# A fused retention and mixture-of-experts layer: two experts' first weights loaded apart, and another order of step 0

## The reference

```python
x = x + attn(_layernorm(x), Wq, Wk, Wv, Wo)    # 8 heads of 16, chunks of 64, decaying state
x = x + ffn(_layernorm(x), Wg, W1, W2)         # 8 experts, hidden 256, the best 2 of each token

# attention, per chunk of 64 tokens and per head
attn = einsum('bhid,bhjd->bhij', qc, kc) * D
o = einsum('bhij,bhje->bhie', attn, vc) + einsum('bhid,bhde->bhie', qc * decay_q, S)
S = decay_s * S + einsum('bhjd,bhje->bhde', kc * decay_k, vc)

# experts, all computed densely, weighted by combine (zero but for two of eight)
h = square(relu(einsum('td,edh->teh', xt, W1)))
y = einsum('teh,ehd->ted', h, W2)
out = einsum('te,ted->td', combine, y)
```

## Time and profile before

| what | us |
|---|---|
| median of three runs | 295.58 |
| lowest and highest | 295.46, 301.28 |
| the profiled execution | 295.8 |
| its span, first to last instruction | 292.9 |
| TensorE busy in the span | 277.2 |
| mean granted clock of TensorE, of full speed | 0.987 |

### The profile page before, as it was taken

The page is one execution under the profiler, slowest core; times in us unless marked ns, Lnnn a source line. Parts: engine busy times, 40 slices in busy tenths (PEclk is TensorE's granted clock), DMA queues, the critical chain, the costliest instruction groups (busy, mean ns, idle before and its releaser), DMA issues.

```text
span 292.9 us, 8869 instructions
## 1 busy us (share of the span) xinstructions
PE 277.2 (95%) x3650; PEld 216.9 (74%) x3650; DVE 219.7 (75%) x569; ACT 176.4 (60%) x253; POOL 190.9 (65%) x152
## 2 busy tenths in 40 slices
PE   7977886999999999999999999999999998999995
PEld 5665465778787778877787777877787787888883
DVE  3746967796569967697569966699569858898883
ACT  2622629646675559746585549756585466686961
POOL 1113595977487786787487785787587874465752
PEclk9997799999999999999999999999999999999999
DMA  7119273004240240604241040304230051305301
GB/s 228 44 24 332 81 248 117 3 0 147 76 135 11 67 157 2 181 0 147 75 121 61 8 186 31 110 2 143 79 102 9 6 165 54 110 8 210 107 0 72
DMA packets 13704, 26.79 MB, mean 91 GB/s; under 512 B 1120, under 2 KB 6752, under 8 KB 13664
## 3 DMA queue, kind: packets, MB, share of 16 engines
q1 hardware_dynamic: 13664, 26.23, 28.0%
HBM read 24.00 MB, written 2.23 MB: 90 GB/s over the span
## 4 chain that ended last, share of the span: by engine, by line
POOL 36%; PE 28%; issue 24%; ACT 5%; DVE 3%; DMA 2%; POOLq 1%; DVEq 0%; ACTq 0%
POOL act_lo L1113 34%; PE h_ps L371 3%; POOL rstd L1085 2%; PE h_ps L373 2%; PE h_ps L372 2%; PE y_ps L398 2%; PE y_ps L392 2%; DMA scale<-w 2%; PE y_ps L393 2%; PE bank L511 1%; PE bank L522 1%; PE bank L432 1%; ACT act_sf L1008 1%; PE h_ps L415 1%; PE y_ps L347 1%
## 5 line engine op out<-in xcount | busy, mean ns | idle before, releaser
L1113 POOL TENSOR_TENSOR act_lo<-act_sf,act_hi 128x512 fp32r<-128x512 f32 x112 | 150.6, 1366 | 54.9 <-ACT act_sf L1008 54.6
L815 DVE SCALAR_TENSOR_TENSOR act_sf<-h_ps,scale 128x1024 f32<-128x1024 f32 x64 | 77.9, 1219 | 47.4 <-PE h_ps L373 21.1
L1001 ACT ACTIVATE act_hi<-act_sf 128x1024 fp32r<-128x1024 f32 x64 | 68.1, 1064 | 56.4 <-DVE act_sf L815 56.3
L1008 ACT ACTIVATE act_sf<-act_sf 128x1024 f32<-128x1024 f32 x64 | 67.3, 1052 | 0.0
L371 PE MATMUL h_ps<-x_hi,w_lo 128*128 128x512 f32 x128 | 54.9, 429 | 0.9 <-ACT act_sf L969 0.9
L373 PE MATMUL h_ps<-x_hi,w_hi 128*128 128x512 f32 x128 | 50.5, 394 | 0.0
L372 PE MATMUL h_ps<-x_lo,w_hi 128*128 128x512 f32 x128 | 50.4, 394 | 0.0
L392 PE MATMUL y_ps<-act_hi,w_lo 128*128 128x512 f32 x112 | 47.0, 420 | 0.0
L393 PE MATMUL y_ps<-act_hi,w_hi 128*128 128x512 f32 x112 | 44.0, 392 | 0.0
L398 PE MATMUL y_ps<-act_lo,w_hi 128*128 128x512 f32 x112 | 35.2, 396 | 0.1
L1085 POOL TENSOR_TENSOR rstd<-variance,minus_half 128x4 f32<-128x4 f32 x16 | 16.1, 1008 | 23.9 <-DVE variance L660 23.8
(11 more groups left out here) (143 smaller groups left out, 424.7 us busy)
## 6 DMA issues: line engine op xcount, KB each, us to landing
scale<-scratch SPq DMA_DIRECT2D x32, 512.0 KB, 4.1
x_t_in<-x_tr SPq DMA_DIRECT2D x8, 256.0 KB, 5.0
x_all<-x SPq DMA_DIRECT2D x8, 256.0 KB, 5.1
out<-out_sb SPq DMA_DIRECT2D x8, 256.0 KB, 4.3
scale<-w SPq DMA_DIRECT2D x1, 1024.0 KB, 5.4
cst<-constants SPq DMA_DIRECT2D x1, 288.0 KB, 4.7
cst<-constants SPq DMA_DIRECT2D x1, 256.0 KB, 2.7
cst<-constants SPq DMA_DIRECT2D x1, 232.0 KB, 5.0
```

Source lines behind the costliest of these rows:

```text
L815: nc.vector.scalar_tensor_tensor(out=act_s[:, u % 2], in0=h_ps[:, u % 2], scalar=0.0, in1=scale[:, f % 2, e].unsqueeze(1).to_broadcast([P, ...
L1001: nc.scalar.activation(act_hi[:, u % 4], act_s[:, u % 2], ACT.Square).then_inc(act_hi_ready, 1)
L1008: nc.scalar.activation(act_f[:, u % 2], act_s[:, u % 2], ACT.Square).then_inc(act_f_ready, 1)
L1113: nc.gpsimd.tensor_tensor(act_lo[:, u % 4, n], act_f[:, u % 2, n], act_hi[:, u % 4, n].bitcast(F32), ALU.subtract).then_inc(pool_low_ready, 1)
```

## The change

The load of `w1` is cut in two: experts 0 and 1 (256 KB) are loaded right behind the first eight loads with a semaphore of their own, `w1_pair_loaded`; the other six (768 KB) where the whole load was. `center_piece(1)` waits for the pair, `center_piece(2)` for the rest. In step 0 alone TensorE runs `transpose_x2(1)` in slot 0, ahead of `project_q(2)` and `project_k(2)`; `transpose_k(2)` in slot 4, behind expert 2's first product and ahead of `project_v(2)`; and `route(1)` in slot 6, behind expert 3's first product. ScalarE runs `high_x(1)` ahead of `mask_q(2)`, and `keep_x(1)` between `square(0)` and `square(1)`.

```diff
-        w1_loaded, w2_loaded = sem("w1_loaded"), sem("w2_loaded")
+        w1_pair_loaded, w1_loaded, w2_loaded = sem("w1_pair_loaded"), sem("w1_loaded"), sem("w2_loaded")
...
             load(1)
 
+            sp.dma_start(w1_in[:, 0:2], w1[0:2].rearrange("e d h -> d e h")).then_inc(w1_pair_loaded, DMA)
             sp.wait_ge(av_done, 1)
-            sp.dma_start(w1_in, w1.rearrange("e d h -> d e h")).then_inc(w1_loaded, DMA)
+            sp.dma_start(w1_in[:, 2:EXPERTS], w1[2:EXPERTS].rearrange("e d h -> d e h")).then_inc(w1_loaded, DMA)
...
                 elif i == 1:
+                    pe.wait_ge(w1_pair_loaded, DMA)
+                elif i == 2:
                     pe.wait_ge(w1_loaded, DMA)
...
-                    if n == 2:
+                    if n == (2 if f >= 1 else 0):
                         transpose_x2(p)
-                    if n == (5 if a < TILES else 4):
+                    if n == (6 if f == 0 else 5 if a < TILES else 4):
                         route(p)
...
-                    if n == 3:
+                    if n == (3 if f >= 1 else 4):
                         transpose_k(a)
...
+                if f == 0:
+                    high_x(p)
                 if a < TILES:
                     mask_q(a)
                 if f == 0:
-                    high_x(p)
                     copy_k(a)
                 square(u)
+                if f == 0:
+                    keep_x(p)
...
                 square(u + 1)
-                if p < TILES:
+                if f >= 1 and p < TILES:
                     keep_x(p)
```

## The result

The changed kernel takes 293.85 us (median of 20 executions, 290.58 to 298.27) against 295.52 of the kernel before on the same chip (20 executions). The ratio is 0.9928, 95% interval 0.9902 to 0.9953: 1.4 to 2.9 us faster, 2.1 at the middle. The forecast was 290.7, 4.9 us faster, with 289.0 to 293.8 as its range. The sign was right, the size was less than half of it, and the time lies just outside the range.

A forecast was written before the change was run, and what follows sets the result against it. TensorE was taken as full after 76 us, with waits to remove in the setup and step 0. Gains of 2.55 and 2.35 summed to 4.9 us, giving 290.7 us, 1.7% faster; range 289.0 to 293.8.

The forecast's parts named there:

- The DMA: Setup: the early pair removes the 1.64 us wait before piece 1, the rest lands in time, other loads lose 0.
- The setup, 2.55 us: Setup: `outputs_within(1)` and expert 0's first product come 2.55 us earlier; bounds 1.0 to 3.3.
- The router's own part, 2.07: Setup: the router's matmuls run at full clock, so its reader starts at 26.25 instead of 28.32, 2.07 us earlier.
- rival A: Setup: the half-speed clock stretch stays, so the front gives 1.0 instead of 2.55 us; 292.2 us, chance 0.2.
- Step 0, 2.35 us: Step 0: the new order removes TensorE's idle waits and the spread begins earlier, gaining 2.35 us; bounds 0 to 2.86.
- POOL does not gain: Step 0: POOL's lows of experts 2 and 3 still end at 58.98; the root follows, ending at 60.65 instead of 61.9.
- slack: Step 0: VectorE's spread began 1.1 us after POOL's root ended; now it would follow at once, 2.35 us earlier in all.
- The main assumption: Behind the setup: the kernel's own semaphores set timing, so TensorE's gain before 71 us carries whole to the end.
- B: Step 0 gives nothing, as ACT's work up to `square(2)` is unchanged and TensorE waits elsewhere; 293.0 us, chance 0.11.
- D: Slower: instruction supply opens new TensorE holes of 1.7 us each; 297.5 us with four, chance 0.03.
- C: More gain: the 1.7 us of "issue" at L522 or POOL's part vanish as well; 289.2 us, chance 0.16.
- E: The change misses: the router still waits for something else and `route(1)` comes no earlier; 295.6 us, chance 0.04.

The follow-up runs named there:

- order only: Changed kernel with the `w1` load whole again, only step 0's new order kept; 294.93 us against 295.36 of the kernel before, ratio 0.9983.
- POOL only: Kernel before (whole load, old order) with POOL's variance root and shares root moved earlier in step 0; 295.88 us against 295.44, ratio 1.0022.
- changed, again: The changed kernel rerun without edit beside its parts; 294.19 us against 295.36 of the kernel before, ratio 0.9953.
- split only: Changed kernel with step 0's old order back, only the two loads of `w1` kept; 293.82 us against 295.36 of the kernel before, ratio 0.995.
- root early: Changed kernel, POOL's variance root ahead of the lows of unit 1 in step 0; 296.51 us against 295.36 of the kernel before, ratio 0.9986.
- shares early: Changed kernel, POOL's root of the shares ahead of the lows of unit 3 in step 0; 293.31 us against 294.89 of the kernel before, 0.9949.
- both early: Changed kernel with POOL's variance root and shares root both moved ahead of lows in step 0; 291.41 us against 294.89 of the kernel before, 0.9874.
- both early, again: The changed kernel with both POOL moves, measured once more; 292.96 us against 295.44 of the kernel before, ratio 0.9905.
- copy early: Both early plus VectorE's copy of tile 0's last state moved from step 0 to the setup; 291.43 us against 294.9 of the kernel before, 0.984.
- fill: Changed kernel plus seven unused matmuls of zeros in TensorE's setup holes; 295.96 us against 294.89 of the kernel before, ratio 1.0014.
- fill and both: Changed kernel plus seven unused matmuls of zeros in the setup and both POOL moves; 293.39 us against 294.89 of the kernel before, 0.9934.
- one fill: Copy early plus one unused matmul of zeros ahead of tile 0's output projection; 294.31 us against 294.9 of the kernel before, ratio 0.9956.

## Why the prediction was right or wrong

Setup and step 0 in the profiles, in us, and the falls of the clock before 71 us (start / length):

| kernel | setup | router ends | step 0 | `state_updates(2)` | falls |
|---|---|---|---|---|---|
| before | 19.09 | 8.49 | 32.34 | 22.57 | 25.9 / 6.8 |
| before, one more profile | 19.17 | 8.46 | 32.70 | 22.58 | 27.7 / 6.8 |
| order only | 19.40 | 8.97 | 31.74 | 22.16 | 27.5 / 6.8 |
| POOL only | 18.95 | 8.34 | 33.51 | 22.61 | 19.9 / 6.8 |
| changed | 17.79 | 7.45 | 31.77 | 22.20 | 21.0 / 3.4 |
| changed, again | 18.43 | 7.52 | 33.50 | 23.90 | 21.1 / 3.4, 34.8 / 6.8 |
| changed, one more profile | 18.67 | 7.55 | 31.76 | 22.17 | 20.0 / 3.4, 33.7 / 3.4 |
| split only | 18.47 | 6.37 | 32.35 | 22.59 | 28.4 / 3.4 |
| root early | 20.50 | 6.37 | 33.08 | 22.08 | 28.1 / 10.2, 62.2 / 3.4 |
| shares early | 16.37 | 6.37 | 31.49 | 21.26 | none |
| both early | 19.62 | 8.34 | 29.79 | 20.00 | 20.1 / 6.8, 30.3 / 3.4 |
| both early, again | 18.85 | 6.37 | 30.87 | 19.99 | 29.4 / 3.4 |
| copy early | 18.32 | 6.37 | 29.74 | 20.00 | 28.2 / 3.4 |
| fill | 18.69 | 6.37 | 33.62 | 23.74 | 38.3 / 3.4 |
| fill and both | 17.86 | 6.37 | 29.97 | 19.98 | none |
| one fill | 18.18 | 6.37 | 29.73 | 20.01 | 28.6 / 3.4 |

(The router's end counts from the end of tile 0's outputs, `state_updates(2)` from the first product of expert 0.)

**The DMA.** Right. No wait for `w` stands ahead of the first piece in any kernel with the split, and piece 2 never waits for the rest, which lands 5.0 us after its issue. The early pair cost the loads around it nothing that these profiles show: the last of the first eight loads lands at 9.4 to 10.3 us in the four profiles with the old load and at 8.9 to 9.9 in the twelve with the pair behind it. So the warning of the Trainium skill (DMA: Bandwidth & Descriptors, Issuing engines are not separate DMA queues) had no price here.

**The setup, 2.55 us.** The mechanism was right, and its size was reached in the one unfilled profile in which the clock stayed full: 2.72 in shares early. The router's own part, 2.07 forecast, measured 2.1 in every profile in which no fall lay ahead of it. What failed is the step "I take 2.55" over "1.0 if the clock still halves through pieces 2 to 4", and with it the weight of rival A (0.2). The DMA wait was not the fall's only cause. With it gone the clock falls at another hole of TensorE: at 20 to 21 us behind the 1.3 to 1.9 us of "issue" at L525, or at 28.1 to 29.4 in or right behind a hole of 1.2 to 1.5 us of "issue" among the matmuls of `state_updates(1)` (shares early, without a fall, has only 0.38 there). Eight of the nine profiles with the new load and no fill have a fall in the setup. Their mean setup, all nine, is 18.56, against 19.15 for the four with the old load: 0.6 us where 2.55 was forecast. The times of split only say 1.5 (0.5 to 2.4). The profiles agree with that if the stretch ahead is counted in: the nine end tile 0's outputs at 19.5 in the mean, the four at 20.6. That stretch goes with the moment of the clock's first rise (last section); whether the early load has a part in it, or chance alone, is not shown. The forecast's evidence against rival A was that the hole at L522 was followed by no fall in one profile. POOL only, with the same code there, has one at 19.9. The hole stands in all sixteen profiles, 1.3 to 1.9 us long, and a fall lies right behind it in five: one profile showed what this hole need not do, not what it doesn't do. What decides it stays open. At L525 the length of the hole does not: falls follow 1.30 to 1.94 us and none follows 1.26 to 1.75.

**Step 0, 2.35 us.** 0.57 measured, 0.60 in order only. All that was said of TensorE and ScalarE held: both waits went, the router (46.70, less 36.61, is 10.1 us behind the first product; before 50.46 - 38.88 = 11.6) came earlier. The step that failed is the sum behind the sentence "POOL does not gain". It let the root follow POOL's lows at once (1.25 us earlier) and the spread follow the root at once (the 1.1 us of "slack"); together 2.35. POOL's lows did end where it said (20.09 us behind the first product, forecast 20.10). But the root then waited 0.93 us for VectorE's shares and came 0.37 earlier, and the slack did not close. Before, then changed:

```profile
60.02 0.17 DVE L787 TENSOR_TENSOR share<-best,r_denom 128x8 f32<-128x8 f32 x1
...
57.39 0.17 DVE L790 TENSOR_TENSOR share<-best,r_denom 128x8 f32<-128x8 f32 x1
...
60.40 0.21 DVE L796 TENSOR_TENSOR spread<-chosen,root 128x64 f32<-128x64 f32 x1
```

In all sixteen profiles the spread starts 1.13 us behind the root's end and 2.85 behind the end of the shares: what stands between them in VectorE's own list (two masks of scores, a `scale_h`, another mask) sets it, not the root. So the step gets what the shares get. The router's sum is read 2.14 us earlier than before, the logits start 1.29 earlier, and the shares end 0.37 earlier. The forecast had not priced this part of the chain, in which POOL holds VectorE twice:

- its variance root, behind the lows of unit 1 in its list, sets when the logits start (1.01 us of wait);
- its lows stop VectorE's short instructions that read two SBUF operands, or copy from SBUF to SBUF, for up to a low: 1.11 for 0.15 (L772), 1.32 or 1.33 for 0.19 (the copy). In the kernel before both ran free, and it was the new order that moved the first of them under the lows. L772 takes 1.10 to 1.13 us in the six profiles in which a low runs at its start and 0.14 to 0.15 in the ten in which POOL is idle. VectorE's timeline of before:

```profile
59.15 0.15 DVE L769 SCALAR_TENSOR_TENSOR denom<-total,best 128x4 f32<-128x4 f32 x1
...
64.39 0.18 DVE L706 COPY update<-state 128x32 f32<-128x32 f32 x1
```

Moving one root alone gives back little (root early 0.12 us at `state_updates(2)`, shares early 0.94, less than half of it kept); both gave 2.20 there, and 2.55 of step 0 from the kernel before (1.5 in the second profile, with the copy held). The gains of the two moves don't add: the first pays only when the second obstacle is gone too. The "shares early" move does not work through an earlier root, but by leaving POOL idle while VectorE chooses.

The held two-input instruction is a rule of the Trainium skill (SBUF — State Buffer, SBUF: two separate sides, and Who interferes with whom): VectorE and GpSimd share a pair of ports as an exclusive lock, the first to start keeps it for its whole instruction, and a VectorE instruction with two SBUF inputs competes with a GpSimd one that reads SBUF. The traces agree: L772 ends within 0.02 us of POOL's last low in the changed kernel, and takes 0.15 where POOL is idle. The copy and the cast read one operand, so that sentence does not cover them; that they are held too is shown by the 1.32 and 1.33 us, which end within 0.05 us of a low's end. The kernel before has a row that could have warned: its logits, only 128x32, take 1.21 us at 55.33, under the lows of the earlier trace rows, and 0.19 in the setup of the changed kernel. In step 0 they take 1.20 to 1.23 in every kernel here, and `combine_r` 1.19 to 1.22 against 0.21 in the setup: their ends lie 0.03 to 0.09 us behind a low's end, so these look like two more holds of 1 us each, which none of the edits touched.

**The sum.** Split 1.5 and order 0.5 by the times of the parts, 2.1 by the whole. The main assumption held: what lies behind step 0 takes 220.3 to 221.8 us in all but three of the profiles, whatever was gained ahead of it. The exceptions (224.0, 225.6, and 223.6 in root early) all have the 1.8 us hole in that stretch, the first two with a fall behind it.

**The rivals.** A (the clock) is what happened in the setup: its 1.0 lies between the 0.6 of the profiles and the 1.5 of the times. With the order's 0.5 that makes the result. B (step 0 gives nothing) nearly happened, but by POOL and VectorE, not ScalarE. D (new holes of "issue") came in part, with none of its size. Where the clock stayed full up to `state_updates(1)` the split brought a hole of 0.4 to 1.5 us there (split only and seven more profiles), which no profile with the old load and none of the three of the changed kernel has. The filled kernels have one more, and a hole of 1.8 us stands near 200 us in one of three profiles of the changed kernel, in none of four with the old load; these are too few to say that the change makes it likelier. That a short supply of instructions makes these holes, as D had it, is not shown. C and E did not happen.

## What to carry to other kernels

Before a chain across engines is priced by the order of one of them, list every instruction of that chain on VectorE, those of other tiles between them too, and see which of POOL's run beside it. Here POOL's order held it and so did POOL's running instructions, and only removing both paid. A gap between an instruction and its input is slack only if nothing else of that engine stands in it. Where a stall is followed by a fall of the clock, count the other holes of the same length around it; taking one away moved the fall here in eight profiles of nine, so forecast the setup at both levels and give the fallen clock most of the weight. And test a reordering with the other engine's order moved too: step 0 gained 0.6 us by the order alone, lost 1.2 by the moves on POOL alone, and gained 2.55 by both.

## What was not expected of the hardware

- **The start differs by 2.5 us between executions.** Tile 0's outputs end at 18.8 to 21.3 us of the span, with the same code. The rows of the same pair in the changed kernel and in shares early:

```profile
5.51 1.12 PE L435 MATMUL bank<-x_t_in,w_center 128*128 128x512 f32 x2 [0.63 <-ACT w_center L927]
```

```profile
6.31 2.07 PE L435 MATMUL bank<-x_t_in,w_center 128*128 128x512 f32 x2 [0.63 <-ACT w_center L927]
```

  The clock had risen by the first and not by the second (2.07 is the pair at half speed). It first rises between 3.9 and 10.7 us of the span.
- **A hole far behind the change can cost more than the change gives.** The 1.8 us of "issue" near 200 us stand in three of the sixteen profiles, in code that none of the kernels alters. The step that holds them takes 34.9 us where the clock stays full and 36.2 to 36.3 where it falls, against 32.85 in the changed kernel: 2.0 and 3.4 us. Over the 20 executions of the changed kernel time and mean clock go together (correlation -0.7), from 290.58 us at 1.0 to 298.27 at 0.974.
- **A fuller TensorE is not a faster one.** With seven added matmuls the clock stayed full through the setup in both profiles, but the time did not fall; 1.2 us of "issue" stand in tile 1's outputs, where no kernel without them has any.
